# Folded FFN2 blocks of a quantized AdaLN feed-forward: partial results copied by ScalarE, biases added in the PSUM banks, products without sums issued first

## The reference, cut to what matters

```python
# x: (4, 1024, 512); F = 2048
fused = concat([x, mean_over_rows(x), cond, cond])         # per row
r = relu(fused @ W + b)                                      # "relation", 512 wide
s_in = max(r) / 255;   rq = clip(round(r / s_in), 0, 255)   # uint8 activations
w1q, w2q = weights rounded to int8, one scale per output row
h = relu(rq @ w1q.T * (s_in * s_w1) + round(b1 / (s_in * s_w1)) * s_in * s_w1)    # (4096, 2048)
s_h = max(h) / 255;    hq = clip(round(h / s_h), 0, 255)
y = (hq @ w2q.T + round(b2 / (s_h * s_w2))) * (s_h * s_w2)                         # (4096, 512)
out = x + y
```

## Time and profile before

| | before |
|---|---|
| median of 3 runs | 321.23 us (320.97 to 321.96) |
| profiled execution, its own time | 321.04 us |
| its span | 319.2 us |
| around the span | 1.84 us |
| granted TensorE clock, mean | 0.998 |
| busy: TensorE, VectorE, ScalarE, GpSimd | 310.8, 272.4, 200.7, 115.0 us |
| instructions | 4733 |

### The profile page before, as it was taken

The page is one execution under the profiler, slowest core; times in us unless marked ns, Lnnn a source line. Parts: engine busy times, 40 slices in busy tenths (PEclk is TensorE's granted clock), DMA queues, the critical chain, the costliest instruction groups (busy, mean ns, idle before and its releaser), DMA issues.

```text
span 319.2 us, 4733 instructions
## 1 busy us (share of the span) xinstructions
PE 310.8 (97%) x1635; PEld 193.3 (61%) x1635; DVE 272.4 (85%) x602; ACT 200.7 (63%) x356; POOL 115.0 (36%) x96
## 2 busy tenths in 40 slices
PE   6999999999999999999999999999999999999995
PEld 6868888888776544444444444444458548647844
DVE  1699988997986699999999999999999698698855
ACT  2435775597386995466665664089959759677400
POOL 1066425634540599992180000710603301400410
PEclk9999999999999999999999999999999999999999
DMA  7999999999973379896990060060999996957952
GB/s 224 205 243 232 226 222 237 259 225 374 282 172 66 70 263 50 342 423 254 424 415 37 6 223 37 35 230 1 367 361 418 408 405 225 402 192 259 341 215 99
DMA packets 51624, 75.57 MB, mean 237 GB/s; under 512 B 20344, under 2 KB 34960, under 8 KB 46864
## 3 DMA queue, kind: packets, MB, share of 16 engines
q1 hardware_dynamic: 51408, 74.99, 78.2%
q10 hardware_dynamic: 192, 0.28, 0.5%
HBM read 45.89 MB, written 25.17 MB: 223 GB/s over the span
## 4 chain that ended last, share of the span: by engine, by line
PE 81%; DVE 11%; DMA 3%; issue 2%; SPq 2%; DVEq 0%
PE bank L589 24%; PE bank L714 21%; PE bank L816 15%; PE bank L826 11%; PE bank L686 6%; DMA x_in<-in_x_dram 3%; DVE hidden L1190 2%; PE bank L701 2%; DVE bank L1320 1%; DVE hidden L1051 1%; DVE bank L1315 1%; DVE hidden L1344 1%; DVE hidden L1342 1%; DVE hidden L1346 1%; DVE hidden L1347 1%
## 5 line engine op out<-in xcount | busy, mean ns | idle before, releaser
L816 PE MATMUL bank<-w_t 128*128 128x512 f16 (+1 forms) x272 | 55.9, 366 | 0.0
L1190 DVE TENSOR_SCALAR_CACHE_REDUCE hidden<-bank,qb,hmax 128x512 f32<-128x512 f32 x62 | 47.6, 806 | 6.4 <-PE bank L714 3.8
L494 POOL TENSOR_TENSOR x_lo<-hidden,x_hi 128x512 fp32r<-128x512 f32 x28 | 35.4, 1303 | 45.6 <-ACT x_hi L910 45.6
L589 PE MATMUL bank<-x_hi,cw_hi 128*128 128x512 f32 x128 | 48.4, 393 | 0.8 <-DVE hidden L1056 0.7
L589 PE MATMUL bank<-x_lo,cw_hi 128*128 128x512 f32 x128 | 48.4, 390 | 0.0
L589 PE MATMUL bank<-x_hi,cw_lo 128*128 128x512 f32 x128 | 48.4, 389 | 0.0
L570 POOL TENSOR_TENSOR pool_r<-pool_r,steps 128x512 f32<-128x512 f32 x16 | 20.2, 1274 | 75.3 <-DVE steps L1367 59.7
L1210 DVE CUSTOM_DVE_ANT_0 hidden<-hidden,bank,hmax 128x512 f32<-128x512 f32 x66 | 45.9, 743 | 0.2
L816 PEld LDWEIGHTS bank<-w_t 128*128 128x128 f16 x272 | 26.6, 98 | 28.3
L1016 ACT ACTIVATE pool_q<-hidden,s_quant 128x512 uint8<-128x512 f32 x63 | 39.1, 710 | 5.2 <-PE bank L826 4.9
L1016 ACT ACTIVATE w_t<-hidden,s_quant 128x512 uint8<-128x512 f32 x56 | 34.7, 709 | 11.7 <-PE bank L816 11.7
(11 more groups left out here) (157 smaller groups left out, 506.2 us busy)
## 6 DMA issues: line engine op xcount, KB each, us to landing
hidden_spill<-hidden SPq DMA_DIRECT2D x16, 1024.0 KB, 9.9
hidden<-hidden_spill SPq DMA_DIRECT2D x16, 1024.0 KB, 10.9
x_in<-in_x_dram SPq DMA_DIRECT2D x32, 256.0 KB, 7.1
pool_r<-in_x_dram SPq DMA_DIRECT2D x8, 1024.0 KB, 5.5
pool_q<-in_L_ffn_w_dram SPq DMA_DIRECT2D x7, 1024.0 KB, 10.2
out_dram<-pool_r SPq DMA_DIRECT2D x7, 1024.0 KB, 8.6
pool_r<-in_L_cond_W_dram SPq DMA_DIRECT2D x2, 1024.0 KB, 9.9
x_in<-in_L_ffn_w_dram SPq DMA_DIRECT2D x1, 1024.0 KB, 5.4
```

The lines of the kernel that those rows point to most:

```text
L494: pool.tensor_tensor(x_lo[:, n % 2, k, :], x_t[:, k, :], x_hi[:, n % 2, k, :].bitcast(F32), ALU.subtract).then_inc(lo_ready, 1)
L589: return pe.matmul(REL[ot][:, :], w[:, k, ot * P:(ot + 1) * P], v[:, n % 2, k, :], start=(k == 0 and w is cw_hi and v is x_hi), stop=(k == ...
L816: return pe.matmul(y_bank[:, cols], hid_q[n % 2][:, ft, j * P:(j + 1) * P], w2_t[:, ft, cols], start=(ft == 0), stop=(ft == FT - 1))
L1190: dve.tensor_scalar(hidden[:, at:at + TB], y_bank[:, :], qb1[:, ft:ft + 1], hmax[:, ft:ft + 1], ALU.add, ALU.max, accum_out=hmax[:, ft:ft ...
```

## The change

ScalarE takes over the six `keep`s of a folded block, as plain copies of 256 columns from the bank to `out_rows`, put between its roundings of the next block (after the 2nd, 4th, 5th, 9th and 11th; two after the 5th). VectorE adds biases inside the banks instead (`bias`: b1a, b1b, and with the difference of two halves of b2, `b2_over`, b5a and b5b), and "c21" (two adds) falls away, since the bank already holds the bias. VectorE has 18 passes in place of 22 in a folded block. The products that need no hidden sums (1a, 1b, 2a) come first, product 2b has a bank of its own (bank 5), and 5b comes before 4a.

```diff
-        F1, F5, F2, FV = (bank[0], bank[3]), bank[1], bank[2], bank[7]
-        PRODUCTS = ("1a", "5a", "6a", "3a", "7a", "2a", "1b", "4a", "5b", "6b", "3b", "7b", "2b", "4b")
+        F1, F2, F5, FV = (bank[0], bank[3]), (bank[2], bank[5]), bank[1], bank[7]
+        PRODUCTS = ("1a", "1b", "2a", "5a", "6a", "3a", "7a", "5b", "4a", "6b", "3b", "7b", "2b", "4b")
+        KEEPS = ("k1a", "k1b", "k5a", "kxa", "k5b", "kxb")
+        TAKES = ("b1a", "b1b", "c11a", "m11a", "b5a", "c12a", "m12a", "c22a", "m22a", "b5b", "m21a", "c12b", "m12b",
+                 "c22b", "m22b", "c11b", "m11b", "m21b")
...
                 part2(0, a11, B11, F1[0], start=True)
+                part2(1, a11, B11, F1[1], start=True)
+                part2(0, a12, B21, F2[0], start=True)
                 pe.wait_ge(hs_ready, sums + 5)
-                part2(0, HS[0], W2S[0], F5, start=True)
-                pe.wait_ge(fold_taken, takes_to(n, "k1a"))
+                part2(0, hs[0], W2S[0], F5, start=True)
+                pe.wait_ge(fold_kept, keeps_to(n, "k1a"))
                 pe.wait_ge(hs_ready, sums + 6)
-                part2(0, HS[1], W2S[1], F1[0])
-                pe.wait_ge(fold_taken, takes_to(n, "k5a"))
+                part2(0, hs[1], W2S[1], F1[0])
+                pe.wait_ge(fold_kept, keeps_to(n, "k5a"))
...
-                part2(0, HS[3], B22, F5)
-                pe.wait_ge(fold_taken, takes_to(n, "kxa"))
+                part2(0, hs[3], B22, F5)
+                pe.wait_ge(fold_kept, keeps_to(n, "kxa"))
...
+                pe.wait_ge(fold_taken, takes_to(n, "m12a"))
+                part2(1, hs[0], W2S[0], F5, start=True)
...
+            def keep(n, name, product, row, cols, r):
+                if product[0] == "6":
+                    act.wait_ge(fold_done, products_to(n, product))
+                else:
+                    act.wait_ge(fold_taken, takes_to(n, "b" + product))
+                act.activation(OUT_ROWS[0][:, row, cols], r[:, FIRST], ACT.Copy).then_inc(fold_kept, 1)
+            def keeps(n, rounded):
+                if rounded == 2:
+                    act.wait_ge(summed, rows_to(BY_POOL[BY_POOL.index(n) - 1]) + TJ)
+                    keep(n, "k1a", "1a", 0, FIRST, F1[0])
+                elif rounded == 4:
+                    keep(n, "k1b", "1b", 1, FIRST, F1[1])
+                elif rounded == 5:
+                    keep(n, "k5a", "5a", 2, LAST, F5)
+                    keep(n, "kxa", "6a", 0, LAST, F1[0])
+                elif rounded == 9:
+                    keep(n, "k5b", "5b", 3, LAST, F5)
+                elif rounded == 11:
+                    keep(n, "kxb", "6b", 1, LAST, F1[1])
...
-            dve.sem_inc(consts_ready, 1)
+            dve.tensor_tensor(b2_over, b2_b[:, LAST], b2_b[:, FIRST], ALU.subtract).then_inc(consts_ready, 1)
...
+            def bias(n, product, r, units):
+                dve.wait_ge(fold_done, products_to(n, product))
+                dve.tensor_tensor(r[:, FIRST], r[:, FIRST], units, ALU.add).then_inc(fold_taken, 1)
...
+                bias(n, "1a", F1[0], b2_b[:, FIRST])
+                if not plain:
+                    sums43(n, 1)
+                elif two:
                     add_bias(n - 1, 2)
+                bias(n, "1b", F1[1], b2_b[:, FIRST])
                 if two:
                     scale_y(n - 1, 2)
+                    add_x(n - 1, 2)
+                elif plain:
                     add_bias(n - 1, 3)
+                result(n, "c11a", "2a", 0, FIRST, F2[0], F2[0], "k1a")
+                bias(n, "5a", F5, b2_over)
                 if two:
                     add_bias(n - 1, 3)
+                elif plain:
                     scale_y(n - 1, 3)
+                result(n, "c12a", "3a", 0, LAST, F5, F5, "kxa")
+                result(n, "c22a", "7a", 2, LAST, F1[0], FV, "k5a")
+                bias(n, "5b", F5, b2_over)
+                ...
+                dve.wait_ge(fold_done, products_to(n, "4a"))
+                scale_row(n, 2, FIRST, F1[0])
```

More of the change, by code:

```diff
@@ L295, in adaln_quantized_ffn, with rows_to @@
         LAST = slice(HALF, TB)
[L298 to L304 removed]
+        F1, F2, F5, FV = (bank[0], bank[3]), (bank[2], bank[5]), bank[1], bank[7]
+        def rows_to(n, row=None):
+            return TJ * BY_POOL.index(n) + (ROWS[n].index(row) + 1 if row is not None else 0)
+        PRODUCTS = ("1a", "1b", "2a", "5a", "6a", "3a", "7a", "5b", "4a", "6b", "3b", "7b", "2b", "4b")
+        KEEPS = ("k1a", "k1b", "k5a", "kxa", "k5b", "kxb")
+        TAKES = ("b1a", "b1b", "c11a", "m11a", "b5a", "c12a", "m12a", "c22a", "m22a", "b5b", "m21a", "c12b", "m12b",
+                 "c22b", "m22b", "c11b", "m11b", "m21b")
+        ROW_TAKES = {0: "m12a", 2: "m21a", 1: "m11b", 3: "m21b"}
         def products_to(n, name=None):
@@ L861, in folded @@
-                pe.wait_ge(fold_taken, takes_to(n, "m11a"))
-                part2(1, a12, B21, F2, start=True)
+                pe.wait_ge(fold_kept, keeps_to(n, "k1b"))
+                part2(1, hs[1], W2S[1], F1[1])
+                pe.wait_ge(fold_kept, keeps_to(n, "k5b"))
+                part2(1, hs[3], B22, F5)
+                pe.wait_ge(fold_kept, keeps_to(n, "kxb"))
+                part2(1, hs[2], W2S[2], F1[1])
+                if n - 1 in PLAIN:
+                    pe.wait_ge(y_taken, plain_to(n - 1, 2))
@@ L863, in folded @@
+                part2(1, a12, B21, F2[1], start=True)
                 pe.wait_ge(fold_taken, takes_to(n, "c22b"))
@@ L1349, in finish_folded, with scale_row @@
+            def scale_row(n, row, cols, r):
+                dve.tensor_tensor(OUT_ROWS[0][:, row, cols], r[:, FIRST], s2_b[:, cols], ALU.mult
+                                  ).then_inc(fold_taken, 1)
             def finish_folded(n):
                 two = n == FOLDED[0]
[L1354 to L1368, removed]
@@ L1375, in finish_folded @@
                 if two:
                     scale_y(n - 1, 2)
-                else:
+                    add_x(n - 1, 2)
+                elif plain:
                     add_bias(n - 1, 3)
-                keep("6a", 0, LAST, F1[0])
-                if two:
-                    add_x(n - 1, 2)
-                result("c12a", "3a", 0, LAST, F5, F5, "kxa")
-                result("c22a", "7a", 2, LAST, F1[0], FV, "k5a")
-                result("c11a", "2a", 0, FIRST, F2, F2, "k1a")
-                keep("1b", 1, FIRST, F1[1])
+                result(n, "c11a", "2a", 0, FIRST, F2[0], F2[0], "k1a")
@@ L1393, in finish_folded @@
                     scale_y(n - 1, 3)
-                else:
+                if plain:
                     add_x(n - 1, 3)
-                keep("6b", 1, LAST, F1[1])
-                if two:
-                    add_x(n - 1, 3)
-                result("c12b", "3b", 1, LAST, F5, F5, "kxb")
-                result("c22b", "7b", 3, LAST, F1[1], FV, "k5b")
-                result("c11b", "2b", 1, FIRST, F2, F2, "k1b")
-                result("c21b", "4b", 3, FIRST, F1[1], F1[1])
+                if n + 1 in FOLDED:
+                    sums12(n + 1, 0)
```

115 lines of the change are left out of this document (70 added, 45 removed).

## The result

The changed kernel takes 324.0 us (median of 5) against 321.02 us (median of 5, 320.95 to 321.96) for the kernel before, measured alongside it; the ratio is 1.0094, with a 95% interval of 1.0068 to 1.0119. It is slower by 0.9%. One of its five executions took 329.52 us in the chip's slower state and is left out of the ratio; the other four took 323.83 to 325.14. Its profiled execution has a span of 322.2 us, 3.0 more than before.

What follows compares the result with a forecast made beforehand. FFN2 was taken to run at TensorE's pace, its waits able to give back 0.60 us. Terms -0.60 + 1.14 + 1.00 + 0.78 + 0.46 = +2.78 us on 321.04 gave 323.8 us, range 322.7 to 326.2.

Steps and rivals of the forecast that it cites:

- b5a and k5a ahead of 3a, block 2: Block 2: VectorE reaches b5a late behind six passes TensorE doesn't need, so 3a starts at 242.27, not 241.13; +1.14 us.
- The same in blocks 4 and 6: Blocks 4 and 6: ScalarE's queue finishes k5a late, so 3a waits 0.50 us in each; +1.00 us.
- 5b ahead of 4a: Each folded block: 5b needs bank 1 and waits for m12a with only 7a between 3a and it; 0.26 each, +0.78 us.
- Roundings before block 7: End of block 6: ScalarE's sixteenth rounding ends late and block 7 waits for all sixteen; +0.46 us once.
- Old wait for k1a: Blocks 4 and 6: 6a now comes four products after 1a, so its 0.30 us wait goes, twice; -0.60 us.
- Price of a copy: ScalarE's new 256-column copy, not in the trace: 0.38 us, and 0.29 from start to start.
- the first rival: ScalarE's copies are dearer or queue worse, 0.60 and 0.50 us each, giving 326.6 us; chance 0.15.
- The second rival: ScalarE is never the late one and VectorE's order alone decides: +1.8 us, 322.8 us; chance 0.12.
- The third: VectorE's load was the bound and fewer passes free it: 320.4 us; chance 0.07 for this or anything within 0.96 us.
- The fourth: The reloads arrive late, costing at most the 3.9 us of the shift, 327.7 us; chance 0.03.
- the fifth: Something outside FFN2 moves with the wider `ident` buffer and gains over 0.96 us; chance 0.02.
- the step on SyncE's queue: Reload 6 and the store and reloads of x behind it all go out 3.9 us later, but stay hidden; costed at nothing.

Runs made afterwards that it cites:

- the first experiment: The changed kernel with six VectorE scalings per folded block, which no product waits for, on 16 columns in place of 256; stage 81.61 us, span 322.2 us.
- the last: The changed kernel with 5a and b5a second, copies moved to fit, bank 6 for 5b and 3b, block 7 tile by tile; 320.74 us.

## Why the prediction was right

Predicted 323.8 us with 0.91 for slower; measured 324.0. Step by step:

- **Ceiling.** "All that a change of its waits can give back is 0.60 us": the version without waits has a stage 0.59 us shorter than before. Shown.
- **b5a and k5a ahead of 3a, block 2**: +1.14 predicted, 1.12 measured; b5a foreseen at 241.38, it started at 241.37. The prediction puts all of it down to the passes ahead of b5a. The moved bias shows that for 0.79 of it; by the trace VectorE's order accounts for 0.89 (b5a could have started at 239.40 + 1.04 + 0.04 = 240.48), and the last 0.23 is product 5a's place, two ahead of 3a. The prediction doesn't name that part; its sum holds it all the same, because it is worked out from when b5a ends.
- **The same in blocks 4 and 6**: 0.50 each predicted, 0.52 measured in block 4; 0.30 of it is shown to be ScalarE's order by the moved copies, and not the passes right ahead of b5a, by two experiments that left block 4 alone. The 0.22 that the prediction leaves to b5a "without the queue" came out too, but b5a waits there for product 5a and not for VectorE's list: the prediction's b5a at 266.50 is also when product 5a is over (262.80 + 2.62 + 1.04 + 0.04), a tie that it doesn't mention.
- **5b ahead of 4a**: 0.26 each, measured 0.28. Shown by the bank of its own.
- **Roundings before block 7**: 0.46 predicted, 0.42 measured. Shown by the tile waits.
- **Old wait for k1a**: gone, as predicted; in the trace after, 5a and 6a take 1.91 us together.
- **Price of a copy**: 0.38 estimated between 0.31 and 0.60; measured:

```profile
L1043 ACT ACTIVATE steps<-bank 128x256 f32<-128x256 f32 x18 | 6.5, 379 | 4.9 <-DVE bank L1412 4.8
```

That removes the first rival (dearer copies). The Trainium skill (ScalarE: Activation LUTs, "What ACT_TABLE_LOAD costs") gave 0.40 us for it, 5% too much here. The second rival (ScalarE is never late) fell in blocks 4 and 6. The third (load) fell with the first experiment and with the last, which has the same passes and no waits. The fourth (late reloads) fell by the trace, as told below; the fifth has nothing for it, since block 1 begins at 222.96 where it began at 222.94. The Trainium skill (VectorE: DVE Perf Modes, "Rules for kernel authors") says to minimize the number of operations in a chain. The runs here limit that to passes that stand ahead of something late: 4.5 us less of passes behind which nobody waited changed nothing, and two short passes ahead of b5a gave 0.48 us.

Three things were less exact. The sum came out at +2.78 where the stage shows +2.90, because blocks 4 and 6 waited 0.83 us each where 0.76 was counted, block 2 1.42 and not 1.40, and block 7 0.42 and not 0.46. Two figures beside the sum don't agree with it: rival 1 takes off 0.55 for the old wait that is 0.60 elsewhere, and the range begins at 322.7 where rival 2's own sum gives 322.8; neither changes a conclusion. And the step on SyncE's queue was too low: I shifted all transfers behind reload 6 by 3.9 us. SyncE's timeline of the changed kernel:

```profile
250.81 4.12 SPq L455 DMA_DIRECT2D hidden<-hidden_spill  x4
...
269.69 0.38 SPq L472 DMA_DIRECT2D pool_r<-in_x_dram  x1
...
289.99 0.51 SPq L464 DMA_DIRECT2D out_dram<-pool_r  x1
...
300.19 0.37 SPq L472 DMA_DIRECT2D pool_r<-in_x_dram  x1
```

Against the earlier trace rows that is 3.9 us for reload 6, 4.5 for the reload of x for block 5 and 6.4 for the last. The last reload waits until the store before it, of block 3, has landed. That store went out 4.5 us later than before (289.99; in the trace of the kernel before 285.48), and the reload followed it after 10.2 us, where it was 8.3. Why the store took longer to land the traces don't show. It stayed hidden: block 7's first add of x started 0.74 us after the scaling before it, with no wait for a transfer. The conclusion held, with 2.5 us less margin than I had counted; some 3 us were left (300.19 + 6.4, the median landing in this trace, against the first add of x at 309.78).

## What to carry to other kernels

Where TensorE is busy without a gap, first work out what all its waits together can give back (here 0.6 of 321 us), and then ask of any new order what stands ahead of each product's turn: a bias of 0.42 us and a copy of 0.38 us let a product wait 1.1 us, 0.9 of it because the bias stood eighth in its engine's list. Moving work to an idle engine puts it behind that engine's own list; give the result that is needed first the first place in every list that it goes through. Look also at how many products stand between the one that makes a result and the one that waits for it: with one between them, a bias and a copy don't fit, wherever they stand in their lists. A product moved earlier takes its cover away from the wait that it used to hide.

## What the runs showed of the hardware

Little that I had not expected: passes, copies and handovers have the same length to 0.01 or 0.02 us from one kernel to the next, so that a hand-made schedule from the traces placed the waits of nine other kernels to within 0.1 us each (the farthest off: 0.78 before 6a in block 4, expected 0.7). Spans came out up to 0.6 us off, in that case 0.44 of it from before block 1. Two copies in a row on ScalarE start 0.28 us apart (two in 0.66 us at 379 ns each), and TensorE's granted clock stayed at 1.00 in every window shown here, through waits of up to 1.1 us.
